# Features of q and k in the order (feature of the head, head), and stacks read in 4 KB runs

## The reference

```python
q = (x @ wq).reshape(B, S, H, HD);  k = ...;  v = ...
p = softmax(einsum("bqhf,bkhf->bhqk", q, k) / sqrt(HD))
o = einsum("bhqk,bkhf->bqhf", p, v).reshape(B, S, D) @ wo
```

## Time and profile before

| | us |
|---|---|
| median of 3 runs | 1781.6 (1781.28 to 1782.33) |
| span of the profiled execution | 1774.2 |
| around that span, against the median | 7.4 |
| TensorE busy in the span | 1538.9 |
| VectorE busy | 1308.8 |
| ScalarE busy | 1142.2 |
| GpSimd busy | 756.7 |
| mean granted TensorE clock | 0.953 |

### The profile page before, as it was taken

The page is one execution under the profiler, slowest core; times in us unless marked ns, Lnnn a source line. Parts: engine busy times, 40 slices in busy tenths (PEclk is TensorE's granted clock), DMA queues, the critical chain, the costliest instruction groups (busy, mean ns, idle before and its releaser), DMA issues.

```text
span 1774.2 us, 44905 instructions
## 1 busy us (share of the span) xinstructions
PE 1538.9 (87%) x14016; PEld 1308.4 (74%) x14016; DVE 1308.8 (74%) x4125; ACT 1142.2 (64%) x2737; POOL 756.7 (43%) x626
## 2 busy tenths in 40 slices
PE   2789999999999998777767767788999999999997
PEld 1578888888888887555655555567888888888876
DVE  2778788788788888776766757777787787877762
ACT  1677667776667666565665656666666766766661
POOL 3345444555445555332222223333445554454423
PEclk8799999999999999998988989899999999999998
DMA  6667655577665578667585766857555665656600
GB/s 137 136 108 98 100 90 100 93 109 99 92 98 92 102 100 127 121 106 109 96 100 90 115 99 109 129 91 107 85 99 78 108 96 80 101 86 103 84 25 13
DMA packets 292307, 173.42 MB, mean 98 GB/s; under 512 B 15696, under 2 KB 291536, under 8 KB 292176
## 3 DMA queue, kind: packets, MB, share of 16 engines
q1 hardware_dynamic: 292176, 171.98, 61.5%
HBM read 121.59 MB, written 50.33 MB: 97 GB/s over the span
## 4 chain that ended last, share of the span: by engine, by line
PE 62%; DMA 13%; DVE 8%; SPq 6%; issue 6%; POOL 3%; ACT 2%; DVEq 0%; ACTq 0%; POOLq 0%
PE d_ps L391 24%; PE t_ps L466 12%; DMA k_stack<-parts 11%; PE d_ps L613 8%; PE s_ps L450 7%; PE o_ps L484 7%; SPq L353 3%; SPq L358 2%; DMA parts<-q_part 2%; PE m_ps L398 2%; PE m_ps L506 2%; DVE prob L790 2%; ACT prob L648 1%; DVE prob_t L936 1%; POOL k_f L972 1%
## 5 line engine op out<-in xcount | busy, mean ns | idle before, releaser
L648 ACT ACTIVATE prob<-prob,neg_max 128x256 f32<-128x256 f32 (+1 forms) x1024 | 435.4, 477 | 285.2 <-DVE neg_max L790 281.7
L466 PE MATMUL t_ps<-ident_sb,prob 128*128 128x128 f32 x2816 | 455.0, 281 | 14.7 <-DVE prob_t L936 13.9
L450 PE MATMUL s_ps<-k_stack,q_stack 96*128 96x256 bf16 (+1 forms) x1536 | 296.1, 276 | 173.0 <-DMA k_stack<-parts 98.6
L466 PEld LDWEIGHTS t_ps<-ident_sb,prob 128*128 128x128 f32 x2816 | 342.8, 145 | 39.7 <-issue 31.3
L450 PEld LDWEIGHTS s_ps<-k_stack,q_stack 96*128 96x128 bf16 x1536 | 105.5, 100 | 290.9 <-issue 120.6
L648 ACT ACTIVATE prob<-s_ps,neg_max 128x256 f32<-128x256 f32 x512 | 216.9, 484 | 108.1 <-DVE neg_max L777 102.2
L936 DVE COPY prob_t<-t_ps 128x512 f32<-128x512 f32 (+1 forms) x384 | 244.9, 638 | 1.4 <-PE t_ps L466 1.4
L790 DVE CUSTOM_DVE_ANT_0 prob<-s_ps,causal 128x128 f32<-128x128 f32 (+1 forms) x512 | 159.2, 351 | 109.4 <-PE s_ps L450 73.4
L790 DVE CUSTOM_DVE_ANT_0 prob<-s_ps,bias_sb 128x256 f32<-128x256 f32 x512 | 193.5, 417 | 60.2 <-PE s_ps L450 50.8
L753 ACT ACTIVATE prob_t<-t_ps 128x512 f32<-128x512 f32 (+1 forms) x384 | 215.9, 562 | 32.0 <-PE t_ps L466 31.6
L972 POOL TENSOR_TENSOR h_lo<-h_f,h_hi 128x512 fp32r<-128x512 f32 x128 | 164.8, 1288 | 131.9 <-DVE h_hi L868 131.9
(11 more groups left out here) (105 smaller groups left out, 3664.9 us busy)
## 6 DMA issues: line engine op xcount, KB each, us to landing
q_stack<-parts SPq DMA_DIRECT2D x288, 128.0 KB, 5.1
k_stack<-parts SPq DMA_DIRECT2D x288, 128.0 KB, 8.9
parts<-q_part SPq DMA_DIRECT2D x96, 192.0 KB, 2.3
parts<-k_part SPq DMA_DIRECT2D x96, 192.0 KB, 2.4
c_in<-ctx SPq DMA_DIRECT2D x32, 256.0 KB, 8.2
x_in<-x_mid SPq DMA_DIRECT2D x32, 256.0 KB, 3.7
x_res<-x_mid SPq DMA_DIRECT2D x32, 256.0 KB, 3.9
x_in<-x SPq DMA_DIRECT2D x16, 256.0 KB, 3.9
```

What stands on the lines that cost most here:

```text
L450: last = mm(s_ps[:, h % 2, q * S:q * S + n], q_stack[:, t.par, h, q * P:(q + 1) * P], k_stack[:, t.par, h, 0:n], start=True, stop=True)
L466: last = nc.tensor.transpose(t_ps[:, h % 2, c:c + P], prob[:, h % 4, q, k * P:(k + 1) * P], ident_sb[:, :])
L648: last = nc.scalar.activation(prob[:, h % 4, q, 0:n], src, ACT.Exp, bias=neg_max[:, h % 4, q:q + 1], scale=-1.0)
```

## The change

The scratch `parts` gets the axes (parity, q or k, part, half m, feature of the head, head of the half, token) in place of (parity, q or k, part, head, feature, token). The columns of the projections' weights for q and k, and the two biases, are permuted on the host by `lanes`, so that within each half of 128 the output partition is `feature * 8 + head` where it was `head * 16 + feature`. The stores write the same rows of 512 bytes (256 tokens in bf16), 384 each. A load of one part reads, for each of the 16 features, 2 runs of 8 heads x 256 tokens x 2 bytes = 4096 bytes, where it read 16 runs of 512 bytes. The number of DMAs, their order, the waits, the destinations and the contents of the stacks are the same.

```diff
-        parts = nc.dram_tensor("parts", (2, 2, 3, H, HD, S), BF16, kind="Internal").ap()
+        parts = nc.dram_tensor("parts", (2, 2, 3, KC, HD, H // KC, S), BF16, kind="Internal").ap()
...
-                        sp.dma_start(parts[t.par, 0, :, m * 8:m * 8 + 8].rearrange("j h d s -> (h d) j s"),
+                        sp.dma_start(parts[t.par, 0, :, m].rearrange("j d h s -> (d h) j s"),
                                      q_part[:, :, m, :]).then_inc(q_written.of(t), 16)
...
-                        sp.dma_start(q_stack[j * HD:(j + 1) * HD, t.par],
-                                     parts[t.par, 0, part].rearrange("h d s -> d h s")).then_inc(stacked.of(t), 16)
+                        sp.dma_start(q_stack[j * HD:(j + 1) * HD, t.par].rearrange("d (m h) s -> d m (h s)", m=KC),
+                                     parts[t.par, 0, part].rearrange("m d h s -> d m (h s)")).then_inc(stacked.of(t), 16)
...
+    lanes = np.arange(D).reshape(KC, H // KC, HD).transpose(0, 2, 1).reshape(-1)
     wa = np.stack([
-        np.stack([l0[n].T for n in ("Wq", "Wk", "Wv", "Wo", "Wg")]),
+        np.stack([l0[n].T[:, lanes] for n in ("Wq", "Wk")] + [l0[n].T for n in ("Wv", "Wo", "Wg")]),
...
-               l1["ln3_s"], l1["ln3_b"], l0["bq"], l0["bk"], l0["b1"], l1["mlp_b1"]]
+               l1["ln3_s"], l1["ln3_b"], l0["bq"][lanes], l0["bk"][lanes], l0["b1"], l1["mlp_b1"]]
```

More of the change, by code:

```diff
@@ L344, in slot @@
                     for m in range(KC):
-                        sp.dma_start(parts[t.par, 1, :, m * 8:m * 8 + 8].rearrange("j h d s -> (h d) j s"),
+                        sp.dma_start(parts[t.par, 1, :, m].rearrange("j d h s -> (d h) j s"),
                                      k_part[:, :, m, :]).then_inc(k_written.of(t), 16)
@@ L357, in slot @@
                     for j, part in enumerate(K_PARTS):
-                        sp.dma_start(k_stack[j * HD:(j + 1) * HD, t.par],
-                                     parts[t.par, 1, part].rearrange("h d s -> d h s")).then_inc(stacked.of(t), 16)
+                        sp.dma_start(k_stack[j * HD:(j + 1) * HD, t.par].rearrange("d (m h) s -> d m (h s)", m=KC),
+                                     parts[t.par, 1, part].rearrange("m d h s -> d m (h s)")).then_inc(stacked.of(t), 16)
                 if h == 12 and has(st.cur, (0,)):
@@ L1041 @@
     none = np.zeros((D, D), np.float32)
+    lanes = np.arange(D).reshape(KC, H // KC, HD).transpose(0, 2, 1).reshape(-1)
     wa = np.stack([
-        np.stack([l0[n].T for n in ("Wq", "Wk", "Wv", "Wo", "Wg")]),
-        np.stack([l1["sa_" + n] for n in ("wq", "wk", "wv", "wo")] + [none]),
-        np.stack([l1["ca_" + n] for n in ("wq", "wk", "wv", "wo")] + [none]),
+        np.stack([l0[n].T[:, lanes] for n in ("Wq", "Wk")] + [l0[n].T for n in ("Wv", "Wo", "Wg")]),
+        np.stack([l1[n][:, lanes] for n in ("sa_wq", "sa_wk")] + [l1["sa_wv"], l1["sa_wo"], none]),
+        np.stack([l1[n][:, lanes] for n in ("ca_wq", "ca_wk")] + [l1["ca_wv"], l1["ca_wo"], none]),
     ])
```

## The result

The changed kernel takes 1722.8 us (median of four runs, 1714.5 to 1732.1), the kernel before 1781.4 beside it: a ratio of 0.968 (95% interval 0.965 to 0.971), 58.7 us less. The forecast was 1776 us with a range of 1725 to 1825; the direction was right, the size was about ten times too small, and the time lies just outside the range. The profiled execution is the slowest of the four (1732.1 us, span 1730.1), so its sums explain 44.1 us of span; the other runs gained somewhat more.

A forecast was written before the change was run, and what follows sets the result against it. TensorE's waits for `k_stack` at 19 sequence starts bound the gain, with loads limited where they land; 0.3 us per start makes 6 us, 1781.6 - 6 = 1776 us, range 1725 to 1825.

The forecast's parts named there:

- What bounds the kernel: TensorE's waits for `k_stack` at sequence starts: 74.9 us in 16 middle-pass waits, 23.7 us in the first three sequences.
- the 19 starts: The 16 middle-pass sequences and the run's first three, where TensorE waits for `k_stack`; each landing gain counts 19 times.
- What limits the loads: Step on the stack loads: limited where data lands, in 16 of 128 partitions, not by reading or packet size.
- the first 0.6 us: Start of the stack loads: 251 GB/s with the same 512-byte packets, before falling to a mean of 130 GB/s.
- the landing side: Main case for the stack loads: 16 neighbouring destination partitions limit them, so almost no gain, 1776 us; chance 0.42.
- I take a quarter, 0.3 us per start: Loading stage: a quarter of the 1.3 us packet saving survives, 0.3 us at each of 19 starts, 6 us.
- the cost per packet is paid in full: Rival on the stack loads: 1.3 us off each of 19 landings, 25 us, 1756 us; chance 0.27.
- slower: the overlap is lost: Rival on the loading stage: engines step in line between 16-partition strips, +1.6 us per start, 1812 us; chance 0.18.
- The issues: Twelve stack-load issues in SP's queue stay: six take 2.85 us, nothing per packet, so 0 us change.
- The clock: TensorE's clock, granted 0.50 in the waits, returns when they go: up to 35 us, total put at 106.
- What lies around the span: The 7.4 us between the profiled span of 1774.2 and the median of 1781.6, carried over unchanged.
- the largest gain: Rival on the stack loads: 512-byte reads are the limit, 91 to 126 us gained, 1675 us; chance 0.13.

The follow-up runs named there:

- ser512: The kernel before (512-byte packets), with SP waiting after each stack load until it has landed: 2622.9 us, single run.
- ser4k: The changed kernel (4 KB packets), with SP waiting after each stack load until it has landed: 2503.2 us, single run.
- a_spread: The changed kernel (4 KB packets) with the stack rows reordered so each load's 16 partitions lie 6 apart: 1684.7 us, ratio 0.948.
- b_spread: The kernel before (512-byte packets) with only the stack rows reordered so each load's 16 partitions lie 6 apart: 1683.6 us, ratio 0.946.
- ord_near: The changed kernel with the six loads of q and of k issued in the order 0, 2, 1, 3, 4, 5: 1747.6 us, ratio 0.981.
- the spread load: A load in the changed kernel with rows 6 apart and SP waiting for each load's landing before the next issue: 2388.7 us, single run.

## Why the prediction was wrong

*What bounds the kernel: right.* The gain is in the waits at the 19 starts, and removing them altogether gave 1774.2 - 1682.1 = 92 us of span, where the prediction had 91 before the clock.

*What limits the loads: right in kind.* The reading of the first 0.6 us, full speed and then slow, pointed to the landing side; the spread rows confirm it, in both packet sizes.

*The step that failed: "I take a quarter, 0.3 us per start".* It measured 2.1 us. Two errors are in it. First, 12.1 us for the stage came from one stage at 130 GB/s; the 16 middle stages run at 107 to 133, median 113.5. The sentence that the changed profile would show 125 to 140 GB/s came true (136), but that was the gain and not the absence of one; `k_stack` landed after 7.2 us, sooner than even the 7.6 that went with a packet cost paid in full. Second, the price of a short packet was taken from packets on a free way: 7 ns of the engine's time, 16 x 7 = 0.11 us per load, and a quarter of it. In the loads alone that difference isn't there: an engine's data packets take 16 x 27 = 0.43 us in `ser512` and 2 x 222 = 0.44 us in `ser4k`. The price is paid at the landing, 0.19 us per load in the queue and 0.21 to 0.23 us for a load alone, of which 0.18 us stand after the last packet. Into spread rows short packets cost nothing that the times show (`a_spread` and `b_spread`, both 2.7 us to the landing), so a limit on the landing side doesn't hide the packets' cost, as I had it, but carries it. So even "the cost per packet is paid in full" (1.3 us per start, 1756 us) was too little. Why a 512-byte packet costs more there isn't settled: a plain cost per packet would make 8 KB at least as good as 4 KB.

*The rival "slower: the overlap is lost" had its sign wrong.* Overlap between strips is real (25 us in `ord_near`), but 4 KB packets did not lose it. An estimate from the single loads: packets and landing behind them, less the 0.40 us of the spread load, are 0.75 + 0.78 = 1.53 us per load with 512 bytes and 0.70 + 0.60 = 1.30 with 4 KB (100 GB/s, the slow phase again), where the queue takes 1.15 and 0.96. The overlap is worth 0.38 and 0.34 us, much the same.

*The issues: nearly right.* Six took 2.67 us in the changed kernel instead of 2.82 (medians); "nothing in that time is per packet" was off by 0.15 us.

*The clock: too high.* I put 15 us of it on a full removal of the waits (106 - 91). In `a_spread` the granted clock rose from 0.953 to 0.980 and TensorE's busy time fell from 1538.9 to 1514.8 us, but the span fell by 92.1 us for 90 us of waits: TensorE's waits for VectorE grew from 92.6 to 110.8 us and those for ScalarE from 27.2 to 30.9, 22 of the 24 us.

*What lies around the span: wrong, without effect.* In every run that has both, time and span differ by about 2 us, not 7.4; the profiled execution of the kernel before was a fast one. The 7.4 us were carried over unchanged and drop out of the forecast of a difference.

*The chances.* 0.13 on the largest gain and the low end at 1725 rested on two cases far apart, with nothing between 1756 and 1675; the truth lay there. The rates of all 16 stages were in the trace before: 1.573/113.5 - 1.573/130 is 1.8 us per start by which the usual stage was slower than the one I used. That wouldn't have shown the cost of the packets, but it would have made room for a gain of this size.

## What to carry to other kernels

Look at where a DMA lands as well as at how long its runs are: a queue of loads into 16 neighbouring partitions ran at 107 to 133 GB/s, and spreading the same loads over partitions six apart, one edit and no new layout in DRAM, was worth 96 us where eight times longer runs were worth 59. Take a rate that carries a sum from every repetition of the stage, not from one. Where a limit is shared, price an edit under that limit and not by its cost on a free path. And place a window inside the stage that it measures: one that runs past the last packet hid the difference between 186 and 258 GB/s.

## What the runs showed of the hardware that was not expected

- The same loads in another order of issue took 25 us more per run (1747.6 against 1722.8).
- The issue of a load costs SP 0.42 to 0.45 us with neighbouring rows and merged runs, 0.59 to 0.61 with rows two or six apart and 0.61 with padded rows (medians; by itself 0.30 with neighbouring rows and 0.55 with rows six apart). With rows six apart the first packet of a single load also starts 0.4 us later (1.34 against 0.93 us after the issue).
- A single 128 KB load into 16 neighbouring partitions moves its packets as fast as one into spread partitions (0.70 and 0.71 us), but lands 1.00 us after its last packet instead of 0.40. Issue to landing shows only 0.15 to 0.2 us of that.
- Runs of 8 KB gave less than runs of 4 KB (1748.0 against 1722.8 us), and 1 KB 1739.7.
